# Early products in a scan, top-2 selection by quarters on two engines, and dummy products ahead of four stages

## What is computed

```python
x = x + conv0(ln(x))        # stages a, o: projections, sigmoid gates, 8 + 8 channel products, norm, projections
t = t + ffn0(ln(t))         # stage b and the scan: Wx, batch norm over 16384 rows, y = sigmoid(Wx_t + y @ V.T)
x = x + conv1(ln(x))        # stages c, z: projections, sigmoid gates, 32 channel products, norm, projection
p, i = top_k(softmax(x @ router_w + router_b), 2)     # stage d: 8 experts
x = x + sum_k p_k / sum(p) * (x @ expert_w[i_k] + expert_b[i_k])
```

## Time and profile before

| | |
|---|---|
| median of 3 runs | 341.1 us (340.87 to 341.93) |
| the profiled execution | 342.12 us; its span 340.4 us |
| busy PE, DVE, ACT, POOL | 236.2, 245.2, 122.5, 102.0 us |
| mean granted clock of TensorE | 0.848 of full speed |
| DMA | 13.08 MB, mean 38 GB/s |

### The profile page before, as it was taken

The page is one execution under the profiler, slowest core; times in us unless marked ns, Lnnn a source line. Parts: engine busy times, 40 slices in busy tenths (PEclk is TensorE's granted clock), DMA queues, the critical chain, the costliest instruction groups (busy, mean ns, idle before and its releaser), DMA issues.

```text
span 340.4 us, 4444 instructions
## 1 busy us (share of the span) xinstructions
PE 236.2 (69%) x1465; PEld 172.8 (51%) x1465; DVE 245.2 (72%) x413; ACT 122.5 (36%) x224; POOL 102.0 (30%) x147
## 2 busy tenths in 40 slices
PE   1288964682395989940978969635649765999993
PEld 1276862451242889830856759524538762332321
DVE  5996849877766000069999743599999599999993
ACT  3343342254223556531445525731324132231110
POOL 4415470587000880000056650001662403030000
PEclk9999995858589699985899989969995555699999
DMA  7100000000000000000000000000005870297611
GB/s 244 28 2 1 2 1 0 2 1 0 0 0 1 2 0 2 0 3 0 0 2 0 2 0 2 1 0 0 2 1 131 202 164 0 55 210 194 160 64 62
DMA packets 6635, 13.08 MB, mean 38 GB/s; under 512 B 2774, under 2 KB 3030, under 8 KB 6614
## 3 DMA queue, kind: packets, MB, share of 16 engines
q1 hardware_dynamic: 6470, 12.81, 14.8%
q10 hardware_dynamic: 144, 0.01, 0.0%
HBM read 2.32 MB, written 2.10 MB: 13 GB/s over the span
## 4 chain that ended last, share of the span: by engine, by line
PE 42%; DVE 41%; issue 6%; POOL 4%; ACT 4%; DMA 1%; SPq 0%; DVEq 0%; POOLq 0%; ACTq 0%
DVE var L318 5%; DVE sums L310 5%; PE ps L1166 4%; PE ps L823 4%; PE ps L1146 4%; PE ps L819 4%; PE ps L525 3%; DVE xn L514 3%; PE ps L1062 2%; DVE xn L1610 2%; PE ps L1076 2%; PE ps L997 2%; DVE gated L1598 2%; PE ps L1158 2%; PE ps L923 2%
## 5 line engine op out<-in xcount | busy, mean ns | idle before, releaser
L525 PE MATMUL ps<-ident,xn 128*128 128x128 f32 x176 | 36.5, 349 | 60.6 <-DVE xn L514 28.3
L525 PEld LDWEIGHTS ps<-ident,xn 128*128 128x128 f32 x176 | 26.2, 181 | 74.4 <-issue 41.5
L704 POOL TENSOR_TENSOR gated<-gated,mask_c x16 | 21.0, 1333 | 54.0 <-DVE gated L1598 54.0
L721 POOL TENSOR_TENSOR x<-x,sg 128x512 f32 x16 | 21.2, 1331 | 42.0 <-DVE sg L1628 40.5
L318 DVE TENSOR_REDUCE var<-squares 128x32 f32<-128x1024 f32 (+1 forms) x24 | 26.9, 1120 | 0.0
L1146 PE MATMUL ps<-gated,pick 96*128 96x512 bf16 x64 | 21.7, 427 | 2.6 <-ACT gated L1372 1.2
L534 ACT ACTIVATE xt<-ps 128x512 f32<-128x512 f32 (+1 forms) x24 | 12.4, 525 | 30.2 <-PE ps L525 30.1
L856 ACT ACTIVATE gated_t<-ps,bn 128x128 f32<-128x128 f32 x56 | 18.0, 366 | 13.1 <-PE ps L823 11.2
L310 DVE TENSOR_REDUCE sums<-x 128x32 f32<-128x1024 f32 x16 | 19.4, 1212 | 3.4 <-DMA x<-in_x_dram 2.0
L314 ACT ACTIVATE squares<-x 128x1024 f32<-128x1024 f32 x16 | 16.8, 1054 | 13.6 <-DVE x L1583 6.3
L823 PE MATMUL ps<-gated_t,v_t 128*128 (+1 forms) x104 | 19.1, 308 | 0.5 <-ACT gated_t L856 0.5
(11 more groups left out here) (245 smaller groups left out, 548.5 us busy)
## 6 DMA issues: line engine op xcount, KB each, us to landing
out_gate<-gated SPq DMA_DIRECT2D x32, 128.0 KB, 2.3
x_copies<-gated SPq DMA_DIRECT2D x32, 128.0 KB, 2.4
x<-in_x_dram SPq DMA_DIRECT2D x4, 512.0 KB, 5.8
out_dram<-x SPq DMA_DIRECT2D x8, 256.0 KB, 2.2
e_full<-in_L_ffn_expert_b_dram SPq DMA_DIRECT2D x12, 1.0 KB
mask_a<-in_L_conv_mask_dram SPq DMA_DIRECT2D x1, 64.0 KB, 7.1
mask_c<-in_L_conv_mask_dram SPq DMA_DIRECT2D x1, 64.0 KB, 1.8
w_x<-in_L_ffn_expert_w_dram SPq DMA_DIRECT2D x1, 32.0 KB
```

The source lines that it names most:

```text
L525: ins = pe.transpose(bank(s)[:, t * P:(t + 1) * P], xn[:, s, t, :], ident[:, :])
L704: pool.tensor_tensor(v, v, m.to_broadcast([P, chans, n]), ALU.mult).then_inc(pj.masked, 1)
L721: pool.tensor_tensor(v, v, sg[:, s, :], ALU.add).then_inc(pj.added, 1)
```

## The change

1. **Scan.** Row 4 of both streams, the first that the first sweep makes, is multiplied with unscaled W (`w_bt`) once seven groups' statistics are in; ScalarE's first sigmoid applies the scale `bn[:, 8:9]` itself. The variance's root goes from ScalarE to nine chained VectorE operations (`root_of` and two more). The second sweep reads the last states in place; its two input products stand ahead of the wait, and ScalarE waits for the copies only before it overwrites them at k = 15.
2. **Dummy products** (`idle_products`): 128x512 bf16 products of ones into a bank nobody reads. Ten in stage o, twelve in b, c and z, behind a wait for the sum of quarter 1 (b: of quarter 3); three, two and six between the products of the batch statistics.
3. **Experts.** Logits by quarters in four banks. VectorE selects for quarters 0 and 1 in 14 steps of 128 x 32 x 8 each. For quarters 2 and 3 ScalarE copies the logits to SBUF, GpSimd makes the elementwise steps (15 operations a quarter), and VectorE only the four maxima (`find_most`), two ahead of the first weighing and six between weighings. Sigmoids replace exponential, addition and reciprocal. Weights are cast and left by quarters, quarter 0's are turned before the last router group. Spread products rotate through three bank pairs (0, 4, 6); sums and the turned weights of quarters 1 to 3 share bank 2, and biases come last in a group. `turn_weights(1..3)` stand in groups 1, 3 and 5.

The diff, cut to what the text speaks of:

```diff
+STEPS = 14
+PICKED = 2
+LOGIT_BANKS = (2, 3, 6, 7)
+FOUND = ((0, 2), (0, 3), (1, 2), (2, 2), (3, 2), (1, 3), (2, 3), (3, 3))
+RANKED = ((0, 2), (1, 2), (0, 3), (2, 2), (1, 3), (2, 3))
...
+PAIRS = (0, 4, 6)
...
+            if q == nm.warned:
+                ins.then_inc(nm.summing, 1)
...
-        n_b = Norm("nb", C, 1.0, EPS_LN, ((0, P),))
+        n_b = Norm("nb", C, 1.0, EPS_LN, ((0, P),), 3)
...
-            return 4 * (q // 2) + 2 * k + q % 2 + 1
+            return 2 * q + k + 1
...
+            def ranked(dst, t, m, q):
+                then(pool, pool.tensor_tensor(of(t, q), of(t, q), each(m, q), ALU.subtract))
+                then(pool, pool.tensor_scalar(of(dst, q), of(t, q), 0.0, None, ALU.is_equal))
+                pool.tensor_tensor(of(dst, q), of(dst, q), ranks, ALU.mult).then_inc(pool_ranked, 1)
...
+                pool.wait_ge(most_found, found_at(q, 1))
+                then(pool, pool.tensor_tensor(of(eq, q), of(eq, q), each(1, q), ALU.subtract))
...
+            def pick_second(q):
+                pool.wait_ge(most_found, found_at(q, 2))
+                then(pool, pool.tensor_tensor(of(pr, q), of(lg, q), each(2, q), ALU.subtract))
+                then(pool, pool.tensor_scalar(of(eq, q), of(pr, q), 0.0, None, ALU.is_equal))
+                pool.tensor_tensor(of(eq, q), of(eq, q), ranks, ALU.mult).then_inc(pool_ranked, 1)
+                pool.wait_ge(d_second, q + 1)
+                then(pool, pool.tensor_tensor(of(sel1, q), of(sel1, q), each(5, q), ALU.mult))
+            def add_second(q):
+                pool.wait_ge(most_found, found_at(q, 3))
+                then(pool, pool.tensor_tensor(of(eq, q), of(eq, q), each(3, q), ALU.subtract))
+                then(pool, pool.tensor_scalar(of(sel2, q), of(eq, q), 0.0, None, ALU.is_equal))
+                then(pool, pool.tensor_tensor(of(sel2, q), of(sel2, q), each(4, q), ALU.mult))
+                pool.tensor_tensor(of(wgt, q), of(sel1, q), of(sel2, q), ALU.add).then_inc(pool_chosen, 1)
+            leave(0)
+            pick_first(2)
+            leave(1)
+            drop_first(2)
+            pick_first(3)
+            pick_second(2)
+            add_second(2)
+            leave(2)
+            drop_first(3)
+            pick_second(3)
+            add_second(3)
+            leave(3)
...
+            if not first:
+                last = y_cm[:, 2 * CHUNK - 1, :]
...
+                    pe.matmul(summed(st, 0, 0), w_bs[:, :], x_cm[:, CHUNK * st, :], start=True, stop=False,
+                              skip_group_check=True)
+                if begun:
+                    begun()
+                pe.matmul(summed(0, 0, 0), v_next[:, :], last, start=False, stop=False, skip_group_check=True)
+                pe.matmul(summed(0, 0, 0)[:, 1:P], v_wrap[:, :], last[:, 0:P - 1], start=False, stop=True,
...
+                pe.matmul(summed(1, 0, 0), v_t[:, :], y_cm[:, CHUNK - 1, :], start=False, stop=True,
...
+                if kept and k == CHUNK - 1:
+                    kept()
...
+            def idle_products(b, n):
+                for _ in range(n):
+                    pe.matmul(bank(b).rearrange("p (k o) -> p k o", o=P), ones_h[:, :],
+                              ones_b[:, :].unsqueeze(1).to_broadcast([P, GROUP, P]), start=True, stop=True,
+                              skip_group_check=True)
...
+            pe.wait_ge(n_o.summing, 1)
+            idle_products(7, 10)
...
+            pe.wait_ge(n_b.summing, 1)
+            idle_products(5, 12)
             groups(pe, turn_group(pe, p_b), wx)
+            pe.wait_ge(p_b.used, GROUPS - 1)
+            for st in range(2):
+                pe.matmul(bank(2 + 2 * st)[:, 0:P], w_bt[:, :], x_cm[:, CHUNK * st + FIRST, :], start=True,
+                          stop=True, skip_group_check=True).then_inc(s_step[st], 1)
+            idle_products(1, 3)
             pe.wait_ge(bn_dve, 1)
-            pe.matmul(bank(4)[:, 0:1], avg4[:, :], mv[:, 0:1], start=True, stop=True).then_inc(bn_pe, 1)
+            pe.matmul(bank(7)[:, 0:1], avg4[:, :], mv[:, 0:1], start=True, stop=True).then_inc(bn_pe, 1)
+            idle_products(1, 2)
             pe.wait_ge(bn_dve, 2)
-            pe.matmul(bank(4)[:, 0:1], avg4[:, :], bn[:, 2:3], start=True, stop=True).then_inc(bn_pe, 1)
+            pe.matmul(bank(7)[:, 0:1], avg4[:, :], bn[:, 2:3], start=True, stop=True).then_inc(bn_pe, 1)
+            idle_products(1, 6)
             pe.wait_ge(bn_dve, 3)
-            pe.matmul(bank(4)[:, 0:P], w_b[:, :, :].rearrange("p s c -> p (s c)"), diag[:, :],
+            pe.matmul(bank(6)[:, 0:P], w_b[:, :, :].rearrange("p s c -> p (s c)"), diag[:, :],
                       start=True, stop=True).then_inc(bn_pe, 1)
...
-            pe.wait_ge(ends_kept, 1)
-            sweep_pe(pe, s_step, s_state, SWEPT)
+            sweep_pe(pe, s_step, s_state, SWEPT, begun=first_swept)
...
+            pe.wait_ge(n_c.summing, 1)
+            idle_products(7, 12)
...
+            pe.wait_ge(n_z.summing, 1)
+            idle_products(6, 12)
...
+                    at = u % 8 * n
+                    ins = pe.matmul(bank(LOGIT_BANKS[u // 8])[:, at:at + n], xd[:, u, :],
                                     w_r[:, :, :].rearrange("p s e -> p (s e)"), start=False, stop=True,
                                     skip_group_check=True)
-                if g % 4 == 3:
+                if g % 2 == 1:
                     ins.then_inc(d_logits, 1)
...
                 pe.wait_ge(w_left, cast_at(q, 1))
                 if q:
                     pe.wait_ge(wt_kept, q)
-                else:
-                    pe.wait_ge(p_d.copied, GROUPS)
+                    pe.wait_ge(q_kept, 2 * q - 1)
                 for t in range(8):
-                    ins = pe.transpose(bank(0).bitcast(BF16)[0:K3, t * P:(t + 1) * P],
+                    ins = pe.transpose(bank(2 if q else 4).bitcast(BF16)[0:K3, t * P:(t + 1) * P],
...
-                if u >= 2:
-                    pe.wait_ge(weighed, u - 1)
+                if u == 0:
+                    pe.wait_ge(p_d.copied, GROUPS)
+                if u == 2:
+                    pe.wait_ge(logits_kept, 2)
+                if u >= 3:
+                    pe.wait_ge(weighed, u - 2)
                 for h in range(2):
-                    ins = pe.matmul(bank(4 + 2 * (s % 2) + h), pick[0:K3, s, h, :],
...
-                if G == 1:
+                if G == 0:
                     pe.wait_ge(chosen, 2)
-                elif G >= 2:
-                    pe.wait_ge(q_kept, G - 1)
+                else:
+                    pe.wait_ge(q_kept, G)
+                    pe.wait_ge(wt_kept, min(QUARTERS, (G + 3) // 2))
                 for k in range(3):
-                    pe.matmul(bank(1 + G % 2), e_bias[0:K3, k, :, :].rearrange("p s c -> p (s c)"),
...
+            pe.wait_ge(x_mid_kept, 1)
+            turn_weights(0)
             router(GROUPS - 1)
-            turn_weights(0)
-            pe.wait_ge(x_mid_kept, 1)
             for G in range(GROUPS):
                 spread_w(G, 0)
-                bias_e(G)
...
-                if G in (0, 2, 4):
-                    turn_weights(1 + G // 2)
+                if G in (1, 3, 5):
+                    turn_weights((G + 1) // 2)
+                bias_e(G)
...
-            act.wait_ge(bn_var, 1)
-            act.activation(bn[:, 4:5], bn[:, 3:4], ACT.Sqrt).then_inc(bn_act, 1)
             act.wait_ge(bn_done, 1)
-            sweep_act(act, s_step, s_state, -FIRST, FIRST)
-            act.wait_ge(ends_kept, 1)
-            sweep_act(act, s_step, s_state, SWEPT)
+            for st in range(2):
+                act.wait_ge(s_step[st], 1)
+                act.activation(y_cm[:, CHUNK * st + FIRST, :], bank(2 + 2 * st)[:, 0:P], ACT.Sigmoid,
+                               bias=bn[:, 9:10], scale=bn[:, 8:9]).then_inc(s_state[st], 1)
+            sweep_act(act, s_step, s_state, -FIRST, FIRST + 1)
+            sweep_act(act, s_step, s_state, SWEPT, kept=lambda: act.wait_ge(ends_kept, 1))
...
+            def weigh_pair(q):
+                if q < PICKED:
+                    act.wait_ge(chosen, STEPS * q + 7)
+                else:
+                    act.wait_ge(most_found, found_at(q, 2))
+                act.activation(quarter(red[:, 4, :], q), quarter(red[:, 2, :], q), ACT.Sigmoid)
+                act.activation(quarter(red[:, 5, :], q), quarter(red[:, 2, :], q), ACT.Sigmoid,
+                               scale=-1.0).then_inc(d_second, 1)
+            def keep_logits(q):
+                act.wait_ge(d_logits, q + 1)
+                act.activation(quarter(lg, q), bank(LOGIT_BANKS[q])[:, 0:QT * EXPERTS]
+                               .rearrange("p (j e) -> p j e", e=EXPERTS), ACT.Copy).then_inc(logits_kept, 1)
...
+                elif q < PICKED:
+                    act.wait_ge(chosen, STEPS * (q + 1))
                 else:
-                    act.wait_ge(chosen, STEPS * (q // 2 + 1))
+                    act.wait_ge(pool_chosen, q - PICKED + 1)
...
```

(87 more changed lines are left out.)

110 lines of the change are left out of this document (59 added, 51 removed).

## The result

The change makes the kernel faster: 330.04 us in the median of 4 runs (328.86 to 331.22) against 340.99 for the kernel before beside it, a ratio of 0.9677 with a 95% interval of 0.9635 to 0.9719. The profiled execution took 331.22 us with a span of 329.5; before, 342.12 and 340.4. The forecast was 328.9. By the ratio the gain is 11.0 us, with some 1.4 to each side; the sum had 12.2.

A forecast was written before the change was run, and what follows sets the result against it. Clock dips cost where TensorE is the chain; VectorE bounds c and z; the scan is product-sigmoid ping-pong, the experts wait on selection. 0.3 + 2.4 + 3.1 + 1.0 + 0 + 5.4 = 12.2: profiled 329.9, median 328.9 us, range 324.8 to 333.6.

The forecast's parts named there:

- Stage o: Ten dummies in stage o lift the clock, so the first sigmoid comes sooner: 0.3 us gained, bounds -0.3 and 1.2.
- Stage b: Twelve dummies ahead of the scan's norm stage put its first two groups at full clock: 2.4 us gained, bounds 1.2 and 2.8.
- The scan's start: Early unscaled product, root on VectorE: row 7's sigmoid 3.1 us sooner, 1.3 of it hanging on the clock; bounds 1.5, 3.4.
- Between the sweeps: TensorE reads the last states in place, input products done before, copies hidden beside the second sweep: 1.0 us gained.
- c and z: Twelve dummies in each stage change nothing, since VectorE bounds both; without its cover, 0.4 lost or 1.5 gained in each.
- Experts: First weighing near 281.0 instead of 286.4, interval to the last addition unchanged at 51: 5.4 us gained, bounds 3.5 and 8.
- The 2.4 us given to the shared bank: Experts, groups 1, 3 and 5: TensorE waits for ScalarE's copy before bias and next spread, 0.8 us each.
- A: Rival: the clock rises no earlier despite dummies, or falls again in the statistics; 333.2 us, chance 0.12.
- B: Rival in the experts: GpSimd's chain a quarter slower than its rows, 6 us longer, 1.5 covered; 333.4 us, chance 0.10.
- C: Rival, slower: GpSimd's operations wait for weighings, delaying quarter 3's weights; 24 us more, 1.3 covered, 352 us, chance 0.04.
- D: Rival in the experts: selection is early, but something else holds the weighings where they were; 5.4 lost, 334.3 us, chance 0.05.
- VectorE idle over 4 us in the last 45: Sign in the experts' last 45 us: VectorE idle over 4 us there would show the forecast wrong.

The follow-up runs named there:

- experiment 1: The changed kernel with none of its 57 dummy products, their waits kept: ratio 0.9771, 7.8 us faster than the kernel before.
- experiment 4: The changed kernel without the twelve dummies ahead of stage b, the eleven of the statistics kept: ratio 0.9738 to the kernel before.
- experiment 3: The changed kernel without the eleven dummies between the batch statistics' products, the twelve of stage b kept: ratio 0.9748 to the kernel before.
- experiment 5: The changed kernel with the scan of before (no early product, root on ScalarE, second sweep from copied ends), dummies and new experts kept: ratio 0.9768.
- experiment 2: The changed kernel without the twelve dummies of stage c and the twelve of stage z: ratio 0.9669 to the kernel before.
- experiment 6: The changed kernel's scan and dummies with the experts of before (halves, all selection on VectorE, two bank pairs): ratio 0.9860, 4.8 us faster than before.
- experiment 7: The changed kernel with turn_weights ahead of the last spread products in groups 1, 3 and 5: ratio 0.9679 to the kernel before.
- experiment 11: The changed kernel with four needless 128x256 GpSimd operations ahead of quarter 3's last ones: ratio 0.9911, 3.0 us faster than the kernel before.

## Why the prediction was right, and where its terms were not

The total and the likeliest case held: 329.9 was said of the profiled execution, 331.2 came, and 2.0 of it is the clock of an untouched stage. That it came so near is in part luck: the profile of the kernel before had the latest rise in stage b of the three without dummies there, and in the scan's start and in the experts' two intervals the parts were off in ways that cancel.

**Stage o**: 0.3 said, 0.24 in the pair. The other profiles with dummies took 32.6 to 33.1 us where the two without took 33.8 and 34.3, so an ordinary pair shows about 1, inside the bound of 1.2. No run left out these ten dummies alone.

**Stage b**: 2.4 said, 2.32 in the pair. The working took the rise at 96.6 as what the kernel before always does. Without dummies it came 3.6, 4.2 and 6.0 us after the first transpose in three executions, so the worth is 1.1 by two of them (experiments 1 and 4), just under the lower bound of 1.2, and 1.9 by the third. A mark read from one execution should have widened the low side.

**The scan's start**: 3.1 said, 3.31 measured, but split the wrong way. The term said 1.8 for the edit and 1.3 for the clock; it is 1.3 for the edit at full clock (9.38 to 8.07) and 2.0 to 2.5 for the clock (experiments 3 and 5). The text shows no working for its 1.3. In the kernel before, the three steps from the first sigmoid (112.9) to that of row 7 took 4.5 us, 1.4 above three steps of 1.04; but with the clock up they take 2.84 (experiment 5), and the table load also comes 0.3 sooner behind the statistics (5.25 us against 5.55). In experiment 3 it had fallen by 109.7, so the product with the diagonal, the first scaled products and two whole steps (1.70 us instead of 0.95) ran at half speed.

**Between the sweeps**: 1.0 said, 0.91 measured. **c and z**: nothing, as said (experiment 2); VectorE is the bound.

**Experts**: 5.4 said, 5.86 measured and 6.1 by experiment 6. The first weighing was said to come 16.1 after the root and came at 15.3; its bound was selection on VectorE (maxima at 274.31, weighing at 274.97). The interval behind it was said to stay at 51 and was 51.4. The 2.4 us given to the shared bank were too many: TensorE does wait 1.2 us for ScalarE's copy in groups 1, 3 and 5, but of VectorE's waits behind it only some 1.1 go when the copy comes sooner (0.80 and 1.07 in groups 4 and 6; 0.19, and 0.40 with 0.19, in experiment 7). Beside it stand a wait of 1.07 for a first projection at half clock and two of 0.35 and 0.68 for GpSimd, which the text had not.

**The rivals.** A (clock not carried) is out; its price of 4.3 us is what experiment 1 lost in the stretches, and 3.2 by the ratios. B and C did not occur, but experiment 11 shows that the text priced them wrongly: it counted a late chain one for one, less its cover, and the loss is more than twice that, since ScalarE's order puts a finished sum behind the late cast and TensorE's clock falls in the wait. C's mechanism, GpSimd slowed by weighings, is not there: its two-input operations took 0.63 to 0.73 us beside weighings, and these took 1.21 to 1.23. D is out: the first weighing moved with the selection.

**The range and the signs.** The lower end, 324.8, does not come out of its own words: the upper bounds of the experts and of b take 3.0 off 328.9, which is 325.9; it takes those of stage o and the scan's start as well. D's own price, 334.3, lies outside the upper end. And one sign of being wrong could not tell anything: VectorE idle over 4 us in the last 45. It was idle 8.7 us there, but 7.3 in the kernel before.

## What to carry to other kernels

A dummy is worth its place only where TensorE itself is the chain right behind it: eleven between the statistics gave 2.5 us, twelve ahead of stage b 1.1 to 1.9, twenty-four ahead of stages bound by VectorE nothing. Price a rise or fall of the clock from several executions, since it moves by microseconds from one to the next. When work goes to an idle engine, look at what other queues hold behind its result: that chain had 0.75 us of slack, and 2.8 us more work on it cost 7.1.
